# First attention in 32 x 32 array tiles, and the last experts of chunks 0 and 1 sorted together, in a one-core four-layer model

## What is computed

```python
qp = elu(einsum('bhcsd,hdf->bhcsf', q, proj)) + 1.0    # c: block of 32 tokens, f: 128 features
kp = elu(einsum('bhcsd,hdf->bhcsf', k, proj)) + 1.0
kv = einsum('bhcsf,bhcsd->bhcfd', kp, v)
num = einsum('bhcsf,bhcfd->bhcsd', qp, kv)
z = 1.0 / (einsum('bhcsf,bhcf->bhcs', qp, kp.sum(axis=3)) + 1e-08)
out = (num * z[..., None]) @ w_out.T + b_out
```

```python
probs = softmax(x @ gate_w); expert_weights, expert_indices = top_k(probs, 2)
expert_weights = expert_weights / expert_weights.sum(-1, keepdims=True)
for i in range(E):
    wi = where(expert_indices == i, expert_weights, 0.0).sum(-1)
    h = silu(x @ w1[i]) * (x @ w3[i])
    out = out + (h @ w2[i]) * wi[..., None]
```

## Time and profile before

| | |
|---|---|
| median of three runs | 1275.29 us |
| profiled execution, its span | 1260.86 us, 1259.1 us |
| TensorE busy, matmul records | 1128.0 us (90%), 5494 |
| VectorE busy | 902.0 us (72%) |
| ScalarE, GpSimd busy | 697.0 us (55%), 510.6 us (41%) |
| mean granted TensorE clock | 0.930 of full |

### The profile page before, as it was taken

One profiled execution on the slowest core, in us unless ns is written; L12 is line 12 of the kernel. 1 busy time (PEld: TensorE's weight loads), 2 busy tenths in 40 slices (PEclk: granted clock), 3 DMA queues, 4 the chain that ended last, 5 costly groups with the idle time before them and its releaser, 6 DMA issues.

```text
span 1259.1 us, 15646 instructions
## 1 busy us (share of the span) xinstructions
PE 1128.0 (90%) x5494; PEld 714.2 (57%) x5494; DVE 902.0 (72%) x2074; ACT 697.0 (55%) x1167; POOL 510.6 (41%) x482
## 2 busy tenths in 40 slices
PE   7999999899999999999999776899998978639977
PEld 6765544355445574655544323597776746318967
DVE  4856437556658857779799998685688799956554
ACT  4575666876735755745676544653424777425221
POOL 2322123212225220065238455663276366584372
PEclk8999999999999879999999875898999989659999
DMA  8500000000000000000000000425323302046673
GB/s 266 194 1 1 1 1 0 1 1 1 1 17 1 1 1 1 18 1 1 1 1 1 0 0 17 149 87 180 126 82 101 109 16 97 16 127 217 236 254 118
DMA packets 39838, 76.86 MB, mean 61 GB/s; under 512 B 3281, under 2 KB 29009, under 8 KB 39249
## 3 DMA queue, kind: packets, MB, share of 16 engines
q0 software_dynamic: 10688, 51.39, 11.9%
q1 hardware_dynamic: 29072, 24.48, 6.1%
HBM read 65.30 MB, written 10.55 MB: 60 GB/s over the span
## 4 chain that ended last, share of the span: by engine, by line
PE 55%; DVE 13%; ACT 11%; POOL 10%; issue 6%; DMA 5%; POOLq 0%; SPq 0%; DVEq 0%; ACTq 0%
PE ps L894 7%; PE ps L2161 5%; PE ps L1469 4%; PE ps L2169 3%; PE ps L1278 2%; DVE own L2027 2%; PE ps L1287 2%; PE ps L668 2%; DMA g_f<-w,slot 2%; PE ps L856 2%; POOL sx L2414 2%; POOL own L2051 2%; PE ps L654 2%; POOL own L2446 1%; PE ps L1589 1%
## 5 line engine op out<-in xcount | busy, mean ns | idle before, releaser
L894 PE MATMUL ps<-own,g_f 128*128 128x512 f32 x320 | 146.1, 597 | 1.1 <-DVE own L1103 1.1
L1221 POOL TENSOR_TENSOR own<-own 128x512 f32<-128x512 f32 x32 | 43.4, 1355 | 162.4 <-PE ps L894 92.1
L894 PEld LDWEIGHTS ps<-own,g_f 128*128 128x128 f32 x320 | 59.1, 191 | 66.8 <-issue 58.4
L2027 DVE TENSOR_TENSOR_SCAN own<-own,carry 128x512 f32<-128x512 f32 x48 | 77.2, 1608 | 20.4 <-POOL own L2051 17.1
L2051 POOL TENSOR_TENSOR own<-own 128x512 f32<-128x512 f32 x32 | 51.9, 1622 | 77.6 <-ACT own L1977 77.6
L1931 PE MATMUL ps<-own,g_c 128*128 128x512 f32 x64 | 45.2, 795 | 40.7 <-POOL own L2057 40.5
L2238 ACT ACTIVATE own<-ps 128x512 f32<-128x512 f32 x60 | 35.7, 596 | 79.6 <-PE ps L2161 79.0
L1968 ACT ACTIVATE own<-own,Acol 128x512 f32<-128x512 f32 x64 | 45.2, 714 | 56.4 <-PE ps L1931 56.2
L2352 DVE TENSOR_TENSOR own<-ps,own 128x512 f32<-128x512 f32 x60 | 41.1, 684 | 47.1 <-PE ps L2161 40.2
L526 ACT ACTIVATE own<-xs,sm 128x128 f32<-128x128 f32 x128 | 52.5, 482 | 31.1 <-POOL sm L518 31.0
L1887 POOL TENSOR_TENSOR own<-own 128x512 f32<-128x512 f32 x32 | 43.6, 1365 | 55.4 <-DVE own L1861 51.7
(11 more groups left out here) (480 smaller groups left out, 3095.3 us busy)
## 6 DMA issues: line engine op xcount, KB each, us to landing
sx<-brow SPq DMA_DIRECT2D x4, 960.0 KB, 10.4
so<-own SPq DMA_DIRECT2D x11, 256.0 KB, 5.0
own<-sx SPq DMA_DIRECT2D x10, 256.0 KB, 4.8
g_l<-p_l SPq DMA_DIRECT2D x1, 2449.0 KB, 13.6
g_f<-p_f SPq DMA_DIRECT2D x1, 2223.5 KB, 9.1
own<-cs SPq DMA_DIRECT2D x8, 256.0 KB, 3.0
g_l<-p_l SPq DMA_DIRECT2D x1, 1866.0 KB, 10.9
g_l<-t_wmod SPq DMA_DIRECT2D x1, 1152.0 KB, 10.3
```

The costliest lines, as they stand in the source:

```text
L894: x = e.matmul(s.bank["V%d%d%d" % (it, k, cc)][:, :], ew2[:, m, 128 * cc:128 * cc + 128], gm, start=False, stop=m == 3)
L1221: e.tensor_tensor(R.gm[m % 2], R.g[m], R.mask[k][m], ALU.mult).then_inc(*s.pool.up("m%d%d%d" % (it, k, m)))
L2027: e.tensor_tensor_scan(H, A, H, init, ALU.mult, ALU.add).then_inc(*s.dve.up("H%d" % n))
```

## The change

Three things are changed, and ORDER is a new string throughout.

First, L1A forms only the 32 x 32 blocks on the diagonal: 16 products of 32 x 32 a head and chunk, each with an output at its own quarter of the partitions, so a tile of 128 rows by 32 columns of the array; the mask becomes a copy of 128 columns; and `mix` is 16 products of 32 rows by 32 columns of the array, with 17 columns moving.

Second, L3F sorts chunks 0 and 1 together. Chunk 0 only picks its experts; chunk 1 ranks and sorts both (16 groups), in TILES[1] = (2048 + 1016) // 128 = 23 tiles, where 15 + 15 were. Chunks 2 and 3 keep 15 each. The tiles' buffers of chunk 1 now lie in T[0] and T[1]. Chunk 0's results are gathered and added by `collected3` and `added3` when the 23 tiles are done.

Third, each `send` and each gather is a piece of its own in ORDER.

```diff
-                    m = e.matmul(tl(p, i), tl(kf, i), tl(qf, i), start=True, stop=True)
+                    for b in range(4):
+                        at = 128 * i + 32 * b
+                        m = e.matmul(p[32 * b:32 * b + 32, 32 * i:32 * i + 32], kf[:, at:at + 32], qf[:, at:at + 32], start=True, stop=True)
...
-                    m = e.matmul(p[:, o:o + 17], tl(b, i), vx[:, i, hd, :], start=True, stop=True)
+                    for k in range(0, 128, 32):
+                        m = e.matmul(p[k:k + 32, o:o + 17], b[k:k + 32, 32 * i:32 * i + 32], vx[k:k + 32, i, hd, :], start=True, stop=True)
...
-                e.tensor_tensor(tile4(T[c][8 + hd % 2]), tile4(s.bank["s%d" % hd][:, :]), V["block"].unsqueeze(1).broadcast_to([128, 4, 128]), ALU.mult).then_inc(*s.dve.up("s%d" % hd))
+                e.tensor_copy(T[c][8 + hd % 2][:, 0:128], s.bank["s%d" % hd][:, 0:128]).then_inc(*s.dve.up("s%d" % hd))
...
+        TILES = [0, (4 * W + 8 * 127) // 128, NJ, NJ]
...
+            if c == 1:
+                q.wait_ge(*ST[7][0].dve("ohb"))
             q.wait_ge(*s.dve("ohb"))
-            b = smb[c]
-            e.matmul(p[:, 0:64], trib[:, :], b[:, :], start=True, stop=False)
...
+            b = smb01[:, :] if c == 1 else smb[c]
+            n = 128 if c == 1 else 64
+            e.matmul(p[:, 0:n], trib[:, :], b, start=True, stop=False)
...
-            for j in range(NJ + 1):
+            for j in range(TILES[c] + 1):
...
+            if c == 0:
+                yield
+                q.wait_ge(*ST[7][1].dve("slot"))
+                yield from collected3(s, q, e)
+                yield
+                return
             q.wait_ge(d_blank[c], 16)
             q.wait_ge(*s.act("xn"))
             if c < LAST:
                 q.wait_ge(*s.dve("slot"))
-                for g in range(8):
-                    send(g)
+                if c == 1:
+                    q.wait_ge(*ST[7][0].act("xn"))
+                for b in ((0, 1) if c == 1 else (c,)):
+                    for g in range(8):
+                        if b != (0 if c == 1 else c) or g:
+                            yield
+                        send(b, g)
```

The new string's first line, which stands for the 41 others:

```diff
-    "tyytyojkkkopopeppplfmaoomaflrrfoalmnqarfqnafnrqoaahsokaaqqkksekkkkfrsgskskkfieacofoeffhoaaaahokkeykaccfkkkaafhdkfckiaaio"
+    "ttyyyojkkokpopepplpfooooaolaqnfqlfmaqqafnmgasfraaraakkkeqksnmkkkffsksrksirrkafdfaaaaiofohddkkakaeefkkffkiicoahaaoocchjhd"
```

More of the change, by code:

```diff
@@ L250, in build @@
         d_sent = [sem(f"d_s{c}") for c in range(NC)]
-        d_rows = [[sem(f"d_l{c}{j}") for j in range(4)] for c in range(NC)]
+        d_rows = [[sem(f"d_l{c}{j}") for j in range(6 if c == 1 else 4)] for c in range(NC)]
         d_out3 = [sem(f"d_o{c}") for c in range(NC)]
@@ L422, in p4_vector @@
             q.wait_ge(*P.pe("bet"))
-            for c in range(NC):
+            for c in range(1, NC):
                 q.wait_ge(d_blank[c], 16)
@@ L2115, in turned @@
                 q.wait_ge(d_rows[c][k], 16)
-                for i in range(over[k]):
-                    m = e.transpose(tl(p, i), tl(later3[k - 2] if c == LAST else T[c][2 + k], i), V["ident"])
+                for i in range(over[c][k]):
+                    m = e.transpose(tl(p, i), tl(later3[k - 2] if c == LAST else ROW3[c][k], i), V["ident"])
                 m.then_inc(*s.pe.up("XT%d" % k))
@@ L2138, in summed @@
                 for i in range(4):
-                    m = e.matmul(tl(p, i), tl(back3[j - LATE], i), tl(T[c][OUT3[j // 4]], j % 4), start=j == LATE and i == 0, stop=j == NJ - 1 and i == 3)
+                    m = e.matmul(tl(p, i), tl(back3[j - LATE], i), tl(OUT3[c][j // 4], j % 4), start=j == LATE and i == 0, stop=j == NJ - 1 and i == 3)
                 m.then_inc(*s.pe.up("Y%d" % j))
             if c < LAST:
-                for k in range(4):
+                for k in range(len(over[c])):
                     yield
@@ L2237, in l3f_scalar, with added3 @@
                         q.wait_ge(*s.dve("b%d" % (j - 2)))
-                    e.activation(T[c][Z3[j % 2]], s.bank["a%d" % j][:, :], ACT.Silu).then_inc(*s.act.up("a%d" % j))
+                    e.activation(Z3[c][j % 2], s.bank["a%d" % j][:, :], ACT.Silu).then_inc(*s.act.up("a%d" % j))
+            yield
+        def added3(s, q, e, w):
+            c = s.c
+            yield
+            q.wait_ge(d_back[c], 128)
+            for i in range(4):
+                xi = xs[:, 4 * c + i, :]
+                e.scalar_tensor_tensor(out=xi, in0=tl(GET3[c][0], i), scalar=w[:, 0, i:i + 1], in1=xi, op0=ALU.mult, op1=ALU.add).then_inc(*s.dve.up("f%d" % i))
+            for i in range(4):
+                xi = xs[:, 4 * c + i, :]
+                yield
+                q.wait_ge(*s.dve("f%d" % i))
+                e.scalar_tensor_tensor(out=xi, in0=tl(GET3[c][1], i), scalar=w[:, 1, i:i + 1], in1=xi, op0=ALU.mult, op1=ALU.add).then_inc(*s.dve.up("x" if i == 3 else "y%d" % i))
             yield
@@ L2430, in l3f_gpsimd @@
                     for g in range(2):
-                        send(2 * (j - 3) + g)
+                        send(c, 2 * (j - 3) + g)
                     yield
                     fetch(j)
-            for j in range(7 if c == LAST else 3, NJ):
+            for j in range(7 if c == LAST else 3, TILES[c]):
                 yield
```

259 lines of the change are left out of this document (139 added, 120 removed).

## The result

Four runs of the changed kernel took 1225.84 to 1237.7 us, median 1233.11; four of the kernel before, taken beside them, 1269.32 to 1275.55, median 1273.16. The ratio is 0.9706, interval [0.9668, 0.9745]: 40 us less, where 20 were forecast. The two traces that are compared here lasted 1260.86 and 1225.84 us, so they show 35 of the 40 us. The ratios are not the quotients of the medians given, and they leave out single executions over 1.5% above the fastest of their kernel, one of 2769.7 us in before_early among them.

The account below looks back on a forecast made before the run. TensorE bounds the start to 549 us and the last 110 us, VectorE leads 549 to 792, then both alternate. 3 + 8 - 28 - 1 - 2 = -20 us from 1275.3 gives 1255 us, range 1230 to 1290.

Parts of the forecast that it names:

- the price of a tile record: First attention's tiles on TensorE: 28 ns a record, so 2048 records total 57.3 us, as before.
- tiles run side by side: Rival for the attention's tiles: 14 ns a record, -28 us, 21 of it before 549 us; 1234 us, chance 0.12.
- The first stretch, +3: Start to 549 us, TensorE leading: its work 542 to 540, plus 5 for shape switches, so +3 us.
- The changes of the array's shape: TensorE switching tile shapes: 62 more changes at 0.09 to 0.12 us each, 5.6 to 7.4 us.
- 549 to 792, +8: Second stretch, VectorE leading: its instructions add 11 us, 8 taken; TensorE's extra 23 us hidden or nearly.
- 792 to 1149, -28: Third stretch: TensorE loses 39 us, VectorE 33; -36 if all is gained, three quarters taken, -28.
- No gain in the third stretch: Rival for 792 to 1149: chunk 3's scans are a chain the experts padded; -8 instead of -28, 1275 us, chance 0.16.
- a wait at L1939 over 60 us: TensorE waiting that long for POOL at chunk 3's L3 attention would show the rival without third-stretch gain right.
- The end, -1: Last 110 us, chunk 3's experts on TensorE: work 90 to 88 us, same tiles behind same sends, -1 us.
- the single sends, -2: Sends as single steps: a pair of chunk 3's POOL steps waits 5 us instead of 10, about -2 us.
- The record at L1285: Sign in first attention: two records 28 ns apart, 32 under 1.1 us; at 38 ns or more the forecast fails.
- the absence of a wait for the sorted rows: First expert tile after the joint sort: about 74 us needed, 75 us of TensorE work covers it; 5.2 us wait goes.

Follow-up runs that it names:

- before_early: Kernel before, with chunk 0's first seven expert tiles cut to stubs of one 8-column product: 1260.66 us, ratio 1.0039.
- after_same: Changed kernel with the tile loops of both attention products turned round, so four products in a row use the same array tile: 1235.78 us, ratio 0.9843.
- after_full: Changed kernel, keeping its joint sort and new order, but with first attention as whole 128 x 128 products and the mask: 1241.9 us, ratio 0.9878.
- before_tiles: Kernel before, in its old order, with only the first attention put in 32 x 32 tiles and the mask made a copy: 1248.6 us, ratio 0.993.
- after_again: Changed kernel run once more, unaltered, against the kernel before: 1218.39 us, ratio 0.9679.

## Why the prediction was wrong, and what in it held

**The step that failed is the price of a tile record.** The working took 28 ns, "nearest to the ranking's 25", so that 2048 records cost the same 57.3 us as before. The runs gave 9 ns when neighbours are different tiles. The two reasons for 28 did not hold: the ranking's 25 ns are no floor of issuing (there every record uses the whole array; 9 ns is issued here), and a load of 25 ns beside a move of 27 is about what one tile needs (23 measured), not four. It is the rival "tiles run side by side" that came true, at 9 instead of its 14 ns; its 1234 us stand beside the measured 1233, which is partly luck: it has -21 us more in the first stretch and keeps the forecast's -20 elsewhere, and the traces have -27 and -8. I had given it 0.12, on one row that had another shape and was not of tiles. The Trainium skill's page "TensorEngine Tiling (Array Packing)", Key Properties, says that different tiles can load and multiply in parallel; this trace agrees, by 9 ns against 23 when the same tile is repeated. The Trainium skill's page "TensorE: Matmul & The Clock Gate", Part 3, says that a load overlaps matmuls in flight only when its row group differs; the scores' tiles share all 128 rows and still follow at 9 ns, so here the measurement disagrees.

after_same shows the size of this one step. With 23 ns a record, near the 28 that I took, the ratio is 0.9843, which on the 1275.3 us of the prediction is 1255.3: the forecast within a microsecond. That agreement is luck: its stretches are -12, +31, -40 and -6, where the sum had +3, +8, -28 and -3. The step to 9 ns is worth 17 us on top of this, against the 20 us by which the forecast fell short; that is measured in the new order only.

**The first stretch, +3, was -27.** The working called that stretch bound by TensorE, and in the new order it paid like one. Three of four chunks' attention stand in it: at 9 ns 2048 records are 18 us instead of 57, 39 us less, of which three quarters are -29; with the sum's +3 that gives -26. The changes of the array's shape cost what was forecast, 0.1 us each: in the kernel after 32 records of L1285 start at 797.67 and L1295 at 798.06, 0.39 us for 0.29 of records. Of the parts, after_full has -4, after_same -12, the kernel after and its like -22 to -27, all against the one trace with 549; against the 538 of before_early each is 11 less. But before_tiles has only -8, within what the same instructions vary by, so the right price alone would not have given the right stretch in every order.

**549 to 792, +8, was +31, and 792 to 1149, -28, was -39.** after_full has +31 and -41 with whole products, so this goes with the new order. I counted the instructions of the two stretches and not what stands in front of whom. Chunk 1's L3A output product stands among chunk 3's attention on TensorE; chunk 3's attention runs in 40 us instead of 68 now that the experts stand behind it. The dividing mark moved; together the two gave -8, not -20.

**No gain in the third stretch.** The rival was nearer for both together than the forecast. In the old order seven tiles less gave nothing (1.0009), and where the tiles were cut early the granted clock was lower and nothing was gained; in the new order putting 18.8 us back costs 6 to 10. Its sign for trouble, a wait at L1939 over 60 us, did not appear.

**The end, -1, and the single sends, -2**, were 0 and within what can be told. The record at L1285, the first stretch and TensorE's busy time missed, and so did the absence of a wait for the sorted rows (2.95 us in the repeat); chunk 1's output at 795, the tail of 110, the 53 products of the up step on VectorE and the sends' 20 us held. Two slips in the working change nothing: the row on a change of shape is in the earlier trace rows, not the earlier trace rows, and three quarters of 36 is 27, not 28.

Open: how much of after_full's 1.2% is the joint sort and how much the new string. Since the joint sort needs another order of pieces, it was not tried alone. Nor is it shown what in the new string keeps TensorE's clock up in the first stretch where the old one, with the same tiles, has less of it. In that stretch neither part shows a gain by itself: 545 with the new order and whole products, 541 with the old order and tiles, both within the 538 to 549 of the kernel before. Only together do they reach 522 to 527.

## What to carry to other kernels

Price an array tile by the distance between records in a queue where neighbouring instructions name different tiles, and write the loops so that they do. Do not count on being paid for removed work, not even in a stretch in which the engine is busy for 95% of the time: the same 39 us of TensorE work were worth 9 us in the old order and some 24 in the new one. With work gone, TensorE's granted clock can be lower too, so read it beside the busy time. In a program whose order is written out by hand, moving one strand by ten places cost some 60 us, more than the whole change gained, so measure an order and do not argue it from sums.

## What the chip showed beyond that

- Float32 products of 32 rows by 32 columns follow each other at 9 ns a record, two records a product, for tiles of 128 x 32 and of 32 x 32 alike (0.46 and 0.44 us for 32); 23 ns in the same tile. That is at a granted clock of 1.00. At 0.50 the same 32 take 0.66 us, 13 to 15 ns a record, depending on how much of the 0.20 us is put down to the modelled end of the last one. From after_again, at 0.50, and from the kernel after, at 1.00:

```profile
808.61 0.66 PE L1285 MATMUL ps<-own 128*32 128x32 f32 x32
...
271.74 0.46 PE L1285 MATMUL ps<-own 128*32 128x32 f32 x32
```

- Those dense records do not keep the clock up. The granted clock in two windows of the kernel after, while chunk 3's attention runs:

```profile
796.00:810.00 14.00, 11.94 (x367) 8.76 (x369) 10.98 (x30) 10.79 (x22) 3.26 (x6) 0.64 0.02 4
810.00:820.00 10.00, 8.31 (x124) 7.01 (x120) 6.61 (x33) 5.08 (x9) 0.00 (x0) 0.50 0.01 2
```

With whole products in the same order (after_full) the clock is 0.90 over chunk 3's attention, 798 to 841 us; with tiles it is 0.71 from 777 to 817. The tiles shortened this attention by 3 us only, from 43 to 40.

- TensorE busy for 97% of 50 us, at 0.53 of its clock, in before_early: a high busy share is no sign of a high clock.
